# Attention kernel with a pipelined step: scores, transposes together, attention last, and one image's phi/g products taken into the start

## The chip, the cores and the metric

The kernel runs on one core of one Trainium2 chip. The metric is the device time of one execution in microseconds (us); the median of three runs of the kernel before is 183.82 us.

## The reference

The input is `x`, four images of 128 channels by 32 x 32 = 1024 pixels, in fp32. Per image:

```
# first block (64 inner channels)
g = Wg x + bg;  theta = Wt x + bt;  phi = Wp x + bp          # 64 x 1024 each
y = ((theta^T phi) / 1024) g^T                               # no softmax
z = x + Wo y^T + bo                                          # 128 x 1024
# second block (128 channels)
t = Wt2 z + bt2;  p = Wp2 z + bp2
attn = softmax(t^T p / sqrt(128))                            # 1024 x 1024, row by row
out = z + Wc (z attn^T) + bc
```

The first block has no softmax, so the kernel multiplies it out as one 128 x 128 matrix per image: `A = I + Wo (g phi^T / 1024) Wt` and an offset `d`, and then z = A x + d. In the second block it uses one matrix U for both projections, and V = Wc z for the values. The row terms `rho` replace the part of the bias that differs between rows.

## The kernel before

**Tiles.** A tile is 128 of the 1024 pixel rows of one image's attention matrix. There are 8 tiles an image and 32 in all (`ALL`), numbered n, with n = 8 b + t. Four tiles make a group, whose 512 columns are attended together into the PSUM bank `numer`.

**Precision.** Products that need nearly full fp32 are made of three fp32r matmuls of hi and lo parts (`three`, L220). Each hi part is written by ScalarE and the lo part is the difference, taken by VectorE after it.

**A tile's way through the engines.** TensorE writes the scores of tile n into `ring` (2 buffers, L296; 6 matmuls of 512 columns). VectorE takes the row maxima (`row_max`, L659). GpSimd adds the row terms (`row_shift`, L794). ScalarE takes the exponentials and their sum (`exps`, L511). VectorE multiplies by the reciprocal of the sum (`norm`, L665). TensorE transposes the tile in two halves of four 128 x 128 blocks (`turn`, L312) into `turned`, two PSUM banks, one per half, with one buffer. ScalarE copies each half as `PT_hi` (`high_turned`, L519), and VectorE writes `PT_lo` (`low_turned`, L673), which frees the half's bank. At last TensorE multiplies the group's tiles with the values, in four pieces of 6 matmuls over the next four steps (`attend`, L322).

**Jobs.** Between these, in the steps of image b, the preparation of image b+1 is made. It is cut into jobs, two a step at most (`job_one`, `job_two`): phi/g products (`pg0`, `pg1`, t = 1), their product `MT` and then `R` (t = 2), `A` and `Z0` (t = 3), `Z1` (t = 4), queries `t0` and values `V0` (t = 5), `V1`, `V2` (t = 6), `t1` (t = 7). All jobs write one PSUM bank, `aux`. The semaphore `aux_free` counts how often it was emptied; a job waits for the count that `aux_before` gives. Copies of `aux` are made by ScalarE, by VectorE, or by both in turn (A, t0, t1, V0 to V2: ScalarE writes the hi part, VectorE then the lo part and frees the bank).

**Order.** The order on each engine is written out by hand; each engine goes through its list strictly, with waits on semaphores. In step n, until n = 30, these are

```
TensorE:  scores(n+2), turn(n,0), job_one, attend piece, turn(n,1), job_two          L433-444
VectorE:  row_max(n+2), low_turned(n-1,1), low_turned(n,0), job_one, norm(n+1), job_two
ScalarE:  high_turned(n,0), job_one, exps(n+2), high_turned(n,1), copy_numer, job_two
GpSimd:   row_shift(n+2), then finish / high_x, low_x, split_z (parts of image b+1)
```

There is no attention in steps 0 to 3, since the first group isn't complete, and no job in image 3's steps (n of 24 and more). `copy_numer` (L528) empties `numer` every fourth step. On GpSimd, `high_x` comes at t = 0, `low_x` at t = 1 and 2, `split_z` at t = 4 and 5, and `finish` at t = 0 and 6; these are ops of 0.6 to 1.5 us. At n = 26 it also makes `V_last`, a 1024-column op.

**The start** (L348 to L394) makes image 0's preparation, with the first products of phi and g in the score ring, and then the scores of tiles 0 and 1; `numer` serves there as a spare bank for two of the three value parts of image 0. The last tile has a way of its own after the loop (L447 to L462).

**Transfers.** SyncE's queue loads the two halves of image 0, the weights, image 1 (L187), and then images 2 and 3 (`load`, L189) once their buffer is free; it then stores the results.

Of the kernel before, what the change touches and what calls it, by code (L numbers as in the profile page):

```python
# [12 lines left out]
IMAGES = 4  # L13
C = 128
# [4 lines left out]
ALL = IMAGES * TILES  # L19
# [31 lines left out]


JOBS = ("pg0", "pg1", "MT", "R", "A", "Z0", "Z1", "t0", "V0", "V1", "V2", "t1")
FIRST_JOBS = ("MT", "R", "A", "t1", "V2")


def aux_before(b, job):

    return len(FIRST_JOBS) + (b - 1) * len(JOBS) + JOBS.index(job) if b else FIRST_JOBS.index(job)

# [4 lines left out]


SPLIT_JOBS = ("A", "t0", "V0", "V1", "V2", "t1")
FIRST_SPLIT = ("t1", "V2")


def high_after(b, job):

    return (len(FIRST_SPLIT) + (b - 1) * len(SPLIT_JOBS) + SPLIT_JOBS.index(job) if b
            else FIRST_SPLIT.index(job)) + 1


def build(nc, x, pg_weights, pg_bias, inner, weights, out):
    with ExitStack() as ctx:
# [103 lines left out]
        def _(sp):  # L182
# [6 lines left out]
            def load(b):  # L189
                if b == 2:  # L190
                    sp.wait_ge(first_z, HALVES)
                else:
                    sp.wait_ge(aux_free, aux_after(b - 2, "pg1"))
                    sp.wait_ge(x_lo, (b - 2) * HALVES)
                sp.dma_start(X[:, b % 2, :], x[b]).then_inc(x_loaded[b], 16)
# [23 lines left out]
        def _(pe):  # L219
# [121 lines left out]
            def attend_last(j):  # L341
# [4 lines left out]
                return mm  # L346

            pe.wait_ge(idle_ready, 1)  # L348
            for _ in range(WARM_UP):
                nc.tensor.matmul(aux[:, 0:C], idle[:, :], idle[:, :], start=True, stop=True)  # L350
            pe.wait_ge(pg_w_loaded, 16)
# [28 lines left out]
            for half in range(HALVES):  # L380
                nc.tensor.matmul(ring[:, 1, columns(half)], AT[:, :], X[:, 0, columns(half)],
                                 start=True, stop=True).then_inc(first_z, 1)

            pe.wait_ge(u_lo, 1)
            pe.wait_ge(first_z_lo, 1)
            queries(0, first_t_bank(0), FIRST_T[0]).then_inc(first_t, 1)
            scores(0)
            pe.wait_ge(first_z_ready, 1)
            pe.wait_ge(vw_ready, 2)
            pe.wait_ge(conv_loaded, 16)  # L390
            value_chunks(0, numer, 0).then_inc(first_v, 1)
            queries(0, first_t_bank(1), FIRST_T[1]).then_inc(first_t, 1)
# [7 lines left out]

            def job_one(b, t):
                if t == 0 and b == 1:
                    first_value_part()
                if t == 1:
                    job_pg(b, 0)
# [12 lines left out]

            def job_two(b, t):
                if t == 0 and b == 1:  # L420
                    job_V(0, 2)
                if t == 1:
                    job_pg(b, 1)
                if t == 2:
                    job_R(b)
                if t == 3:
                    job_Z(b, 0)
                if t == 5:
                    job_V(b, 0)
                if t == 6:  # L430
                    job_V(b, 2)

            for n in range(ALL - 1):  # L433
                b, t = divmod(n, TILES)
                if n + 2 < ALL:
                    scores(n + 2)
                turn(n, 0)
                if b + 1 < IMAGES:
                    job_one(b + 1, t)
                if n >= GT:  # L440
                    attend(n // GT - 1, n % GT)
                turn(n, 1)
                if b + 1 < IMAGES:
                    job_two(b + 1, t)
            attend(ALL_GROUPS - 2, PIECES - 1)
# [20 lines left out]
        def _(act):  # L466
# [99 lines left out]

            def job_one(b, t):
                if t == 0 and b == 1:
# [13 lines left out]

            def job_two(b, t):
                if t == 0 and b == 1:
# [10 lines left out]
            for n in range(ALL - 1):  # L595
                b, t = divmod(n, TILES)
                high_turned(n, 0)
                if b + 1 < IMAGES:
                    job_one(b + 1, t)
                if n + 2 < ALL:  # L600
                    exps(n + 2)
                high_turned(n, 1)
                if n >= GT and n % GT == GT - 1:
                    copy_numer(n // GT - 1)
                if b + 1 < IMAGES:
                    job_two(b + 1, t)
            copy_numer(ALL_GROUPS - 2)
# [6 lines left out]
        def _(dve):  # L614
# [105 lines left out]
            first_z_low(1)  # L720
            first_t_low(0)
            row_max(0)
            dve.wait_ge(u_copied, 1)
# [6 lines left out]

            def job_one(b, t):
                if t == 0 and b == 1:
                    first_row_terms(1)
                    first_v_low(1)
                if t == 1:
                    make_pg(b, 0)
# [8 lines left out]

            def job_two(b, t):
                if t == 0 and b == 1:
                    low_V(0, 2)
                if t == 1:
                    make_pg(b, 1)  # L750
# [17 lines left out]
            low_turned(ALL - 2, 1)  # L768
            dve.wait_ge(turned_ready, ALL * HALVES)
# [117 lines left out]
```

## Time and profile before

| | |
|---|---|
| runs | 184.03, 182.73, 183.82 us; median 183.82 |
| the profiled execution | 183.74 us; its span 181.9 us, so 1.8 us lie around the span |
| mean granted TensorE clock | 0.991 |
| TensorE busy | 168.2 us, 92% |
| VectorE busy | 132.8 us, 73% |
| ScalarE busy | 98.0 us, 54% |
| GpSimd busy | 49.6 us, 27% |

A matmul's listed duration covers its whole way through the array and overlaps the next one's; the distance between the starts of two rows says what it costs TensorE. "Busy" therefore says little about slack; idle time in brackets at a row, with what ended it, says more.

### The profile page before, as it was taken

The page shows a single profiled execution, that of the slowest core. Times are in us where ns is not written, and L with a number is a line of the kernel's source. Part 1 is how long each engine was busy: PE and PEld are TensorE (multiplying, and loading weights), DVE is VectorE, ACT ScalarE, POOL GpSimd, SP SyncE. Part 2 cuts the span into 40 slices and gives each one's busy share as a digit, 9 for nine tenths or more (in the row PEclk, how much of TensorE's full clock was granted, in tenths as well). Part 3 has the DMA queues.
Part 4 walks back from the last instruction along what each step waited for, and adds up shares of the span by engine and source line. Part 5 has one row for each costly group of instructions (what it writes and reads, how often), then busy time and mean ns, then how long its engine had stood idle before and what let it go on. Part 6 is the DMA issues. An engine that isn't in the chain of part 4 may idle for free.

```text
span 181.9 us, 2601 instructions
## 1 busy us (share of the span) xinstructions
PE 168.2 (92%) x967; PEld 135.3 (74%) x967; DVE 132.8 (73%) x217; ACT 98.0 (54%) x178; POOL 49.6 (27%) x73
## 2 busy tenths in 40 slices
PE   7896896797999999999999999999999999898994
PEld 6755684675787878878787878788787867675794
DVE  1313697776999888756988889766988988988612
ACT  3032546357676665347666755557655856576320
POOL 1015012330440036210443063301523042403020
PEclk9997899999999999999999999999999999999999
DMA  4603000011000001000001010000001010000111
GB/s 133 184 0 115 0 4 0 0 48 73 0 2 0 0 4 58 0 0 4 0 0 58 0 49 14 0 0 0 4 0 61 0 58 4 0 0 0 58 61 58
DMA packets 2829, 4.76 MB, mean 26 GB/s; under 512 B 448, under 2 KB 1280, under 8 KB 2816
## 3 DMA queue, kind: packets, MB, share of 16 engines
q1 hardware_dynamic: 2304, 4.39, 6.9%
q10 hardware_dynamic: 512, 0.20, 0.6%
q8 instruction: 8, 0.13, 0.3%
q14 instruction: 5, 0.04, 0.1%
HBM read 2.49 MB, written 2.10 MB: 25 GB/s over the span
## 4 chain that ended last, share of the span: by engine, by line
PE 70%; DVE 23%; ACT 2%; DMA 2%; issue 1%; ACTq 0%
PE numer L337 14%; PE turned L318 11%; DVE negmax L662 10%; PE ring L223 8%; PE ring L225 8%; PE ring L224 8%; DVE PT_lo L677 7%; PE aux L229 3%; PE aux L282 3%; PE aux L344 2%; DMA pg_w<-pg_weights_dram 2%; PE aux L223 2%; DVE P L670 2%; PE ring L229 2%; PE aux L235 2%; PE aux L224 2%
## 5 line engine op out<-in xcount | busy, mean ns | idle before, releaser
L524 ACT ACTIVATE PT_hi<-turned 128x512 fp32r<-128x512 f32 x62 | 37.0, 596 | 40.0 <-PE turned L318 39.7
L662 DVE TENSOR_REDUCE negmax<-ring 128x1 f32<-128x1024 f32 x32 | 39.2, 1223 | 21.8 <-PE ring L225 21.2
L318 PE MATMUL turned<-identity,P 128*128 128x128 f32 x256 | 39.1, 276 | 5.5 <-DVE P L670 3.1
L318 PEld LDWEIGHTS turned<-identity,P 128*128 128x128 f32 x256 | 30.5, 140 | 17.5 <-DVE PT_lo L677 5.9
L516 ACT ACTIVATE P<-ring,shift 128x1024 f32<-128x1024 f32 x32 | 35.7, 1116 | 13.1 <-POOL shift L803 12.8
L803 POOL TENSOR_SCALAR shift<-negmax,rho 128x1 f32<-128x1 f32 x32 | 11.8, 368 | 106.4 <-DVE negmax L662 103.1
L677 DVE TENSOR_TENSOR PT_lo<-turned,PT_hi 128x512 fp32r<-128x512 f32 x62 | 39.8, 681 | 1.0 <-ACT PT_hi L524 0.9
L670 DVE TENSOR_SCALAR P<-P,rden 128x1024 f32<-128x1024 f32 x32 | 30.6, 957 | 1.1
L223 PE MATMUL ring<-Z_hi,t_hi 128*128 128x512 f32 x64 | 28.0, 438 | 1.5 <-DVE t_lo L707 1.5
L225 PE MATMUL ring<-Z_lo,t_hi 128*128 128x512 f32 x64 | 25.7, 402 | 0.0
L224 PE MATMUL ring<-Z_hi,t_lo 128*128 128x512 f32 x64 | 25.6, 400 | 0.0
L337 PE MATMUL numer<-PT_hi,V_hi 128*128 128x512 f32 x56 | 23.8, 424 | 0.0
L337 PE MATMUL numer<-PT_hi,V_lo 128*128 128x512 f32 x56 | 22.1, 395 | 0.0
L337 PE MATMUL numer<-PT_lo,V_hi 128*128 128x512 f32 x56 | 22.1, 395 | 0.0
L223 PEld LDWEIGHTS ring<-Z_hi,t_hi 128*128 128x128 f32 x64 | 12.2, 191 | 4.3 <-DVE t_lo L707 2.1
L225 PEld LDWEIGHTS ring<-Z_lo,t_hi 128*128 128x128 f32 x64 | 12.3, 192 | 2.9
L224 PEld LDWEIGHTS ring<-Z_hi,t_lo 128*128 128x128 f32 x64 | 12.3, 192 | 1.7
L337 PEld LDWEIGHTS numer<-PT_hi,V_lo 128*128 128x128 f32 x56 | 10.5, 188 | 2.5
L337 PEld LDWEIGHTS numer<-PT_hi,V_hi 128*128 128x128 f32 x56 | 10.6, 188 | 1.8
L337 PEld LDWEIGHTS numer<-PT_lo,V_hi 128*128 128x128 f32 x56 | 10.6, 189 | 1.6
L830 POOL TENSOR_TENSOR result<-attended,Z 128x512 f32<-128x512 f32 x7 | 9.0, 1287 | 5.4 <-ACT attended L534 5.4
L282 PE MATMUL aux<-VW,Z 128*128 128x130 f32 x52 | 8.1, 287 | 0.5 <-DVE V_lo L649 0.5
(113 smaller groups left out, 198.6 us busy)
## 6 DMA issues: line engine op xcount, KB each, us to landing
out_dram<-result SPq DMA_DIRECT2D x7, 256.0 KB, 2.0
X<-x_dram SPq DMA_DIRECT2D x3, 512.0 KB, 3.2
X<-x_dram SPq DMA_DIRECT2D x2, 256.0 KB, 4.1
out_dram<-result SPq DMA_DIRECT2D x1, 192.0 KB, 1.9
w<-weights_dram SPq DMA_DIRECT2D x1, 128.0 KB, 5.5
wi<-inner_dram ACTq DMA_DIRECT2D x1, 64.2 KB, 5.6
pg_w<-pg_weights_dram ACTq DMA_DIRECT2D x1, 64.0 KB, 3.6
pg_b<-pg_bias_dram ACTq DMA_DIRECT2D x1, 64.0 KB, 5.2
```

The costliest lines, as they stand in the source:

```text
L223: nc.tensor.matmul(to, left_hi, right_hi[:, cols], start=first, stop=False)
L224: nc.tensor.matmul(to, left_lo, right_hi[:, cols], start=False, stop=False)
L225: return nc.tensor.matmul(to, left_hi, right_lo[:, cols], start=False, stop=last)
L282: mm = nc.tensor.matmul(bank[:, at:at + V_COLS], Z[:, b % Z_BUFFERS, j * TILE:(j + 1) * TILE], VW[:, :], start=True, stop=True)
L318: mm = nc.tensor.transpose(turned[:, j * TILE:(j + 1) * TILE], P[:, n % P_BUFFERS, j * TILE:(j + 1) * TILE], identity[:, :])
L337: mm = nc.tensor.matmul(numer[:, :], left[:, b % 2, chunk], right[:, g, j, :], start=(j == 0 and n == 0), stop=(j == TILES - 1 and n == 2))
L516: nc.scalar.activation(P[:, n % P_BUFFERS, :], ring[:, n % 2, :], ACT.Exp, bias=shift[:, t:t + 1], accum_out=den[:, t:t + 1]).then_inc(pro ...
L524: nc.scalar.activation(PT_hi[:, group % GROUPS, half_chunks(half), k * TILE:(k + 1) * TILE], turned[:, columns(half)].rearrange("p (j r) - ...
L662: nc.vector.tensor_reduce(negmax[:, t:t + 1], ring[:, n % 2, :], AX.X, ALU.max, negate=True).then_inc(max_ready, 1)
L670: nc.vector.tensor_scalar(P[:, n % P_BUFFERS, :], P[:, n % P_BUFFERS, :], rden[:, t:t + 1], None, ALU.mult).then_inc(probs_normed, 1)
L677: nc.vector.tensor_tensor(PT_lo[:, group % GROUPS, half_chunks(half), rows], turned[:, columns(half)].rearrange("p (j r) -> p j r", j=CHUN ...
L803: nc.gpsimd.tensor_scalar(shift[:, t:t + 1], negmax[:, t:t + 1], rho[:, b % 2, t:t + 1], rho[:, b % 2, t:t + 1], ALU.subtract, ALU.add).th ...
```

## The change

In each step TensorE now makes scores(n+2), the first job, both halves of turn(n), the second job, and the attention piece last. VectorE makes row_max(n+2), the first job, norm(n+1), low_turned(n,0), the second job and low_turned(n,1). ScalarE makes the first job, both halves of high_turned(n), the second job and exps(n+2); copy_numer moved from the end of one step to the beginning of the next. GpSimd's program is the same.

Image 1's phi/g products leave step 1. Their first half is issued on TensorE after image 0's Z products, ahead of the first queries; the second half goes to the bank `numer`, between the first queries and scores(0). VectorE copies both (`make_pg(1, 0)`, `copy_pg`) between `first_t_low(0)` and `row_max(0)`. The numbering of the jobs is now a list, in which (1, pg0) stands behind (0, A); a value part that writes `numer` waits for the copy. The load of image 3 waits on the renamed counts. WARM_UP stays; `keep_warm` is only its loop as a function.

```diff
+AUX_ORDER = ([(0, "MT"), (0, "R"), (0, "A"), (1, "pg0"), (0, "t1"), (0, "V2")] + [(1, job) for job in JOBS[2:]]
+             + [(b, job) for b in range(2, IMAGES) for job in JOBS])
+SPLIT_ORDER = [(b, job) for b, job in AUX_ORDER if job in ("t0", "V0", "V1", "V2", "t1") or (job == "A" and b)]
...
# SyncE, load(3)
-                    sp.wait_ge(aux_free, aux_after(b - 2, "pg1"))
+                    sp.wait_ge(first_pg_copied, HALVES + 1)
+                    sp.wait_ge(aux_free, aux_after(1, "pg0"))
...
# TensorE, start
+            job_pg(1, 0)
             pe.wait_ge(u_lo, 1)
             pe.wait_ge(first_z_lo, 1)
             queries(0, first_t_bank(0), FIRST_T[0]).then_inc(first_t, 1)
+            phi_g_chunks(1, numer, 1).then_inc(first_pg, 1)
             scores(0)
...
+            pe.wait_ge(first_pg_copied, HALVES + 1)
             value_chunks(0, numer, 0).then_inc(first_v, 1)
...
# TensorE, step
                     scores(n + 2)
+                if b + 1 < IMAGES:
+                    early_job(b + 1, t)
                 turn(n, 0)
+                turn(n, 1)
                 if b + 1 < IMAGES:
-                    job_one(b + 1, t)
+                    late_job(b + 1, t)
                 if n >= GT:
                     attend(n // GT - 1, n % GT)
-                turn(n, 1)
-                if b + 1 < IMAGES:
-                    job_two(b + 1, t)
...
# ScalarE, step
+                if n >= 2 * GT and n % GT == 0:
+                    copy_numer(n // GT - 2)
+                if b + 1 < IMAGES:
+                    early_job(b + 1, t)
                 high_turned(n, 0)
+                high_turned(n, 1)
                 if b + 1 < IMAGES:
-                    job_one(b + 1, t)
+                    late_job(b + 1, t)
                 if n + 2 < ALL:
                     exps(n + 2)
-                high_turned(n, 1)
-                if n >= GT and n % GT == GT - 1:
-                    copy_numer(n // GT - 1)
-                if b + 1 < IMAGES:
-                    job_two(b + 1, t)
...
# VectorE, start
             first_t_low(0)
+            make_pg(1, 0)
+            dve.wait_ge(first_pg, HALVES + 1)
+            copy_pg(numer[:, :], 1, first_pg_copied)
             row_max(0)
...
# VectorE, step
                     row_max(n + 2)
-                if n >= 1:
-                    low_turned(n - 1, 1)
+                if b + 1 < IMAGES:
+                    early_job(b + 1, t)
+                norm(n + 1)
                 low_turned(n, 0)
                 if b + 1 < IMAGES:
-                    job_one(b + 1, t)
-                norm(n + 1)
-                if b + 1 < IMAGES:
-                    job_two(b + 1, t)
+                    late_job(b + 1, t)
+                low_turned(n, 1)
```

The jobs are the same as before under new names (`early_job` for `job_one`, `late_job` for `job_two`), except that phi/g is made only for b > 1.

## Rows read from the trace of the kernel before

**Rows 1.** The page: the chain that ended last, shares by engine.
```profile
PE 70%; DVE 23%; ACT 2%; DMA 2%; issue 1%; ACTq 0%
```
**Rows 2.** Busy time by stretch: image 1's eight steps, then step 26.
```profile
63.47:103.13 39.66, 39.42 (x231) 32.02 (x230) 32.28 (x53) 24.46 (x45) 13.10 (x17) 1.00 0.04 14
...
150.70:154.66 3.96, 3.89 (x23) 2.96 (x22) 3.23 (x6) 2.36 (x5) 0.96 (x2) 1.00 0.01 4
```
**Rows 3.** Timeline of step 8, which has no job: start, duration, instruction, [idle before].
```profile
63.47 0.48 PE L223 MATMUL ring<-Z_hi,t_hi 128*128 128x512 f32 x1
...
64.94 0.60 PE L318 MATMUL turned<-identity,P 128*128 128x128 f32 x4
65.13 1.23 DVE L662 TENSOR_REDUCE negmax<-ring 128x1 f32<-128x1024 f32 x1 [0.41 <-PE ring L225]
65.29 0.48 PE L337 MATMUL numer<-PT_hi,V_hi 128*128 128x512 f32 x1
...
65.63 0.60 ACT L524 ACTIVATE PT_hi<-turned 128x512 fp32r<-128x512 f32 x1 [0.70 <-PE turned L318]
...
66.27 1.28 DVE L677 TENSOR_TENSOR PT_lo<-turned,PT_hi 128x512 fp32r<-128x512 f32 x2
...
66.46 0.37 POOL L803 TENSOR_SCALAR shift<-negmax,rho 128x1 f32<-128x1 f32 x1 [3.98 <-DVE negmax L662]
...
67.01 0.66 PE L318 MATMUL turned<-identity,P 128*128 128x128 f32 x4
67.42 0.48 PE L223 MATMUL ring<-Z_hi,t_hi 128*128 128x512 f32 x1
```
**Rows 4.** Busy time by stretch, the start: columns PE, PEld, DVE, ACT, POOL, PEclk, DMA.
```profile
9.00:11.50 2.50, 2.30 (x18) 1.93 (x18) 0.42 (x1) 0.76 (x4) 0.00 (x0) 1.00 0.00 0
...
12.50:15.80 3.30, 1.54 (x7) 0.60 (x5) 1.85 (x3) 1.74 (x3) 1.96 (x4) 1.00 0.37 129
15.79:19.44 3.65, 3.64 (x12) 3.05 (x13) 0.85 (x1) 0.00 (x0) 1.02 (x1) 0.53 0.07 29
```
**Rows 5.** Timeline of the start: scores(0), the first value part, the next queries.
```profile
15.80 0.62 PE L223 MATMUL ring<-Z_hi,t_hi 128*128 128x512 f32 x1 [0.90 <-DVE t_lo L707]
...
18.35 1.37 PE L282 MATMUL numer<-VW,Z 128*128 128x130 f32 x6
...
19.47 0.42 PE L223 MATMUL turned<-Z_hi,UT_hi 128*128 128x384 f32 x1
```
**Rows 6.** Timeline of step 1, TensorE with its waits.
```profile
29.58 0.66 PE L318 MATMUL turned<-identity,P 128*128 128x128 f32 x4 [1.30 <-DVE P L670]
...
30.57 1.16 PE L229 MATMUL aux<-pg_w,X 128*128 128x128 f32 x8 [0.33 <-DVE V_lo L649]
```
**Rows 7.** Busy time by stretch: steps 1, 2 and 3.
```profile
26.66:34.40 7.74, 5.00 (x33) 3.74 (x32) 6.57 (x14) 4.67 (x10) 2.96 (x4) 1.00 0.00 0
34.40:38.90 4.50, 4.10 (x36) 3.15 (x34) 3.48 (x6) 1.85 (x4) 1.50 (x2) 1.00 0.00 0
38.90:44.14 5.24, 4.12 (x25) 3.35 (x25) 4.16 (x8) 3.35 (x9) 0.47 (x2) 1.00 0.32 105
```
**Rows 8.** Timeline of step 13: t0's hi and lo copies, then V0.
```profile
91.08 0.69 ACT L496 ACTIVATE t_hi<-aux,U 128x512 fp32r<-128x512 f32 x1
...
92.08 0.74 DVE L638 SCALAR_TENSOR_TENSOR t_lo<-aux,U,t_hi 128x512 fp32r<-128x512 f32 x1
...
92.88 0.94 PE L282 MATMUL aux<-VW,Z 128*128 128x130 f32 x6
...
93.57 0.48 PE L223 MATMUL ring<-Z_hi,t_hi 128*128 128x512 f32 x1
```
**Rows 9.** Busy time by stretch: steps 13 and 14.
```profile
88.07:93.57 5.50, 5.50 (x33) 4.22 (x31) 5.36 (x7) 3.86 (x8) 3.24 (x4) 1.00 0.00 0
93.57:98.77 5.20, 5.04 (x33) 4.18 (x32) 4.53 (x10) 3.25 (x6) 1.62 (x2) 1.00 0.00 0
```
**Rows 10.** Timeline of step 12: a GpSimd op and VectorE's norm beside it.
```profile
87.80 1.29 POOL L822 TENSOR_TENSOR Z_lo<-Z,Z_hi 128x512 fp32r<-128x512 f32 x1
...
87.92 1.72 DVE L670 TENSOR_SCALAR P<-P,rden 128x1024 f32<-128x1024 f32 x1
```
**Rows 11.** Busy time by stretch: step 27, then steps 29 and 30.
```profile
154.66:159.34 4.68, 3.90 (x24) 2.96 (x22) 4.64 (x7) 2.42 (x5) 2.19 (x2) 1.00 0.00 0
163.30:172.40 9.10, 8.03 (x43) 5.92 (x41) 7.29 (x13) 4.75 (x9) 1.60 (x2) 1.00 0.07 29
```
**Rows 12.** The tile P: VectorE's norm, min/median/max ns.
```profile
L670 DVE TENSOR_SCALAR P<-P,rden x32: 752/754/2122, 22.2 to 170.6; 128x1024 f32<-128x1024 f32 x32
```

More of the change, by code:

```diff
@@ L53 @@
 JOBS = ("pg0", "pg1", "MT", "R", "A", "Z0", "Z1", "t0", "V0", "V1", "V2", "t1")
-FIRST_JOBS = ("MT", "R", "A", "t1", "V2")
+AUX_ORDER = ([(0, "MT"), (0, "R"), (0, "A"), (1, "pg0"), (0, "t1"), (0, "V2")] + [(1, job) for job in JOBS[2:]]
+             + [(b, job) for b in range(2, IMAGES) for job in JOBS])
+SPLIT_ORDER = [(b, job) for b, job in AUX_ORDER if job in ("t0", "V0", "V1", "V2", "t1") or (job == "A" and b)]
 def aux_before(b, job):
-    return len(FIRST_JOBS) + (b - 1) * len(JOBS) + JOBS.index(job) if b else FIRST_JOBS.index(job)
+    return AUX_ORDER.index((b, job))
 def aux_after(b, job):
     return aux_before(b, job) + 1
-SPLIT_JOBS = ("A", "t0", "V0", "V1", "V2", "t1")
-FIRST_SPLIT = ("t1", "V2")
 def high_after(b, job):
-    return (len(FIRST_SPLIT) + (b - 1) * len(SPLIT_JOBS) + SPLIT_JOBS.index(job) if b
-            else FIRST_SPLIT.index(job)) + 1
+    return SPLIT_ORDER.index((b, job)) + 1
 def build(nc, x, pg_weights, pg_bias, inner, weights, out):
@@ L346, in attend_last, with keep_warm @@
                 return mm
+            def keep_warm(to, count):
+                for _ in range(count):
+                    nc.tensor.matmul(to, idle[:, :], idle[:, :], start=True, stop=True)
             pe.wait_ge(idle_ready, 1)
-            for _ in range(WARM_UP):
-                nc.tensor.matmul(aux[:, 0:C], idle[:, :], idle[:, :], start=True, stop=True)
+            keep_warm(aux[:, 0:C], WARM_UP)
             pe.wait_ge(pg_w_loaded, 16)
@@ L399, in first_value_part, with early_job @@
                 value_chunks(0, numer, 1).then_inc(first_v, 1)
-            def job_one(b, t):
+            def early_job(b, t):
                 if t == 0 and b == 1:
                     first_value_part()
-                if t == 1:
+                if t == 1 and b > 1:
                     job_pg(b, 0)
@@ L417, in job_one, with late_job @@
                     job_t(b, 1)
-            def job_two(b, t):
+            def late_job(b, t):
                 if t == 0 and b == 1:
                     job_V(0, 2)
-                if t == 1:
+                if t == 1 and b > 1:
                     job_pg(b, 1)
@@ L565, in _, with early_job @@
             exps(1)
-            def job_one(b, t):
+            def early_job(b, t):
                 if t == 0 and b == 1:
@@ L581, in job_one, with late_job @@
                     high_t(b, 1)
-            def job_two(b, t):
+            def late_job(b, t):
                 if t == 0 and b == 1:
@@ L729, in _, with early_job @@
             low_t(0, 1)
-            def job_one(b, t):
+            def early_job(b, t):
                 if t == 0 and b == 1:
@@ L734, in job_one @@
                     first_v_low(1)
-                if t == 1:
+                if t == 1 and b > 1:
                     make_pg(b, 0)
@@ L744, in job_one, with late_job @@
                     low_t(b, 1)
-            def job_two(b, t):
+            def late_job(b, t):
                 if t == 0 and b == 1:
                     low_V(0, 2)
-                if t == 1:
+                if t == 1 and b > 1:
                     make_pg(b, 1)
@@ L759, in _ @@
                     row_max(n + 2)
-                if n >= 1:
-                    low_turned(n - 1, 1)
+                if b + 1 < IMAGES:
+                    early_job(b + 1, t)
+                norm(n + 1)
                 low_turned(n, 0)
                 if b + 1 < IMAGES:
-                    job_one(b + 1, t)
-                norm(n + 1)
-                if b + 1 < IMAGES:
-                    job_two(b + 1, t)
-            low_turned(ALL - 2, 1)
+                    late_job(b + 1, t)
+                low_turned(n, 1)
             dve.wait_ge(turned_ready, ALL * HALVES)
```

## The prediction

> **What bounds the kernel now.** I read the chain of waits first, then busy time by stretch, then the timelines. The chain is 70% TensorE and 23% VectorE [rows 1]: look for where VectorE comes in. In image 1's eight steps TensorE was idle 0.24 of 39.66 us [rows 2]; image 2 repeats them. No order can gain there except by packing matmuls closer. The idle time lies at both ends: steps 1 to 3 have 2.74, 0.40 and 1.12 us [rows 7], the start runs partly at the low clock [rows 4], and image 3's steps, which have no jobs, are paced by VectorE [rows 2, 11].
>
> **A step without jobs.** In step 8 scores take 1.47 us (63.47 to 64.94), a half of the transposes 0.35, attention again 1.47, to 66.76; then turn(n,1) waits until 67.01 [rows 3], because low_turned(n-1,1) stands behind row_max(n+2) on VectorE. The work is 3.95 - 0.25 = 3.7 us. In the new order tile n's lo copies end in step n. With S the start of scores: row maximum at S+1.6 (1.66 here, less the changeover after transposes), norm from S+2.8, to 3.7, lo copies to 4.3 and 4.95; the next transposes start at S+3.7+1.4 = 5.1, and their second half at 5.5. So TensorE waits for nothing. VectorE needs 1.14 + 0.95 + 2 x 0.6 = 3.3 us a step [rows 3, 12], less than 3.7. The step becomes 3.7, as TensorE's work is unchanged.
>
> **Image 3 and the end.** Steps 24, 25, 26 and 28 take 3.96 each, alike within 0.01 [rows 2], 27 takes 4.68, 29 and 30 together 9.10 [rows 11]: 29.62 us. New: 5 x 3.7 = 18.5. From step 29, counted from S: its work ends at 3.7; turn(30) waits for tile 29's lo copies (4.3 and 4.95), ends at 5.35, and 12 attention matmuls (2 x 1.47, less a changeover) end at 8.2. That is 26.7, a gain of **2.9**. Step 8 and step 16 gain 0.25 each.
>
> **Steps with two jobs.** This is the price. The second job needs `aux` empty. Before, turn(n,0)'s remainder, attention and a half of the transposes lay between the jobs; now only eight transposes, 0.85 us, and attention is queued behind the waiting job. Also row_max(n+2) stands ahead of the first job's copy on VectorE. At t = 5: t0 is issued S+1.4 to 2.07, ScalarE's copy follows 2.3 to 3.0 (0.69), VectorE's 3.05 to 3.8 (0.74) [rows 8]; transposes end at 2.95, V0 starts at 3.85, so TensorE idles 0.9. V0 takes 0.69 (92.88 to 93.57), attention 1.4: 5.93 against 5.50, **+0.43** [rows 8, 9]. At t = 6 V1's copies (0.5 and 0.8 us, from 2.4 and 2.9) let V2 go at 3.7: 5.65 against 5.20, **+0.45** [rows 9]. At t = 1 pg0's copy waits for row_max until 2.75 and takes 0.7; pg1 goes at 3.45, 0.35 late; the step is 5.8, +0.15. At t = 2 MT and R need ScalarE alone, which is free early: -0.1. At t = 3 AT_lo is ready at 3.1, 0.2 late, which the two changeovers saved pay for: 0. One job at t = 4 and 7: 0. Image 1 then costs 39.66 + 0.15 - 0.1 + 0.43 + 0.45 - 0.25 = 40.35, **+0.7**, image 2 the same: **+1.4**. In steps 4 to 7 of image 0 it is **+0.9**. VectorE's backlog after t = 5 (its last lo copy ends near S+7.1 to 7.5) is gone before the next row maximum at 5.93+1.6.
>
> **Steps 0 to 3.** Times here are on the old trace's scale. In step 0 the value part moves before the transposes and the step grows by 0.5: scores(3) starts at 27.1 instead of 26.66. VectorE's list gives row_max(2) 25.5 to 26.7, value part to 28.05, norm(1) to 29.0, lo copies of tile 0 at 29.6 and 30.7 (V2's copy between). So turn(1,0) starts at 29.65, 1.1 us idle, against 29.58 before [rows 6], but turn(1,1) follows at 30.75 with no phi/g products (16 matmuls, two lots of 0.85) and no copies between, and scores(4) starts at 31.25 instead of 34.40: -3.15. Step 2 is 3.8 (old 4.50), bounded by TensorE; step 3 is 4.6 against 5.24, as AT_lo stands behind a VectorE list that is 1.2 us late and Z0 waits 0.85 for it. By scores(6): 39.65 against 44.14, so **-4.4**.
>
> **The start.** All loads are in: the DMA share is 0.00 from 9.00 to 11.50 [rows 4], so image 1 is there. Two times eight passes of 0.11 us go into the 1.76 us that TensorE idles in 12.50 to 15.80 [rows 4]: the first lot 13.15 to 14.25, ahead of queries at 14.37; the second 14.75 to 15.65, ahead of scores(0) at 15.80 [rows 5]. Tight, up to 0.1 late. VectorE's two copies (1.4 us) lie between 15.74 and row_max(0). They cost nothing in their cover; without it the 0.7 us of the second would show in V's wait. More matters: after the thinly used stretch (1.54 busy of 3.30) the clock fell, and was 0.53 in 15.79 to 19.44, the 1.2 GHz level [rows 4]. There scores(0) took 2.55 (15.80 to 18.35) and the value part 1.12 [rows 5], against 1.4 and 0.69 at 2.4 GHz [rows 3, 8]: 1.6 us. With the gap two thirds filled I take it that the clock stays up: **-1.5**; if it falls anyway, 0. The Trainium skill (TensorE: Matmul & The Clock Gate, "The HAM clock gate") has the fall follow an idle window; the trace agrees only in part, since the engine was busy nearly half of the time ahead of the fall. By it the gain would stand as well.
>
> **The sum.** -4.4 + 0.9 + 1.4 - 2.9 - 1.5 = -6.5. The profiled execution took 183.74 us, 0.08 under the median of 183.82; 183.82 - 6.5 = **177.3**, the forecast.
>
> **Unknown: norm beside GpSimd.** A norm lasts 0.75 us, but 1.72 when a GpSimd op of 1.29 us began just ahead of it [rows 10, 12]. Before, row_shift and norm stood apart; now both are released by the end of row_max, within 0.1 us of each other, and GpSimd's longer ops follow row_shift directly. If norm gets in first, shift is late by up to 0.75, which exps, at the end of ScalarE's list, can bear: 0. If GpSimd keeps its turn, norm is late by 0.37, or by 0.37 + 1.29. I take the first, since nothing held norm in step 8, with a third of the norms at risk as the bound.
> The Trainium skill (GPSIMD Engine Reference, "Specifications") says that the two engines share SBUF interfaces and contend when VectorE runs in a two-port mode; the trace agrees (1.72 against 0.75), and this rule speaks against the change.
>
> **Rivals.**
> - *The clock falls anyway* (free of the filling): 177.3 + 1.5 = 178.8. For it: the fall came after a partly busy stretch. Chance 0.15.
> - *Second jobs wait longer than walked.* I count 2.2 us of waits an image at t = 1, 3, 5 and 6. If VectorE comes to each first job 0.3 to 0.5 late, 11 such steps add 3.3 to 5.5: 180.6 to 182.8. For it: VectorE has 5.36 us of work in step 13 [rows 9]. Chance 0.15, half of it above 182.
> - *Slower: GpSimd holds norm.* Place: norm behind row_shift and the op after it, in t = 0, 1, 2, 4, 5 and 6 of three images, 18 steps. Price 1.66 each on VectorE, of which a light step absorbs 0.4; up to 1 us a step reaches TensorE, +18. It decides from 6.5/18 = 0.36 us a step; beyond 0.46 the kernel is slower than 185.7. Against it: the second ops were mostly off norm's path, and waits for jobs absorb some. Chance 0.08, near 187.
> - *More gained:* the waits of second jobs are covered by packing, under 175.5. Chance 0.07.
>
> **The numbers.** The forecast's own case has 0.55 and spans 175.6 to 179.5. The range from 175.5 to 181.5 takes in the clock case and the lower half of the waits case; about 0.2 is left out. About 1% (182.0 and 185.7) is what a measurement can tell from no change. Faster: 0.55 + 0.15 + 0.07 + half of 0.15 = 0.84. Same: 0.08. Slower: 0.08.
>
> **What would show it.** In the changed kernel's profile: PEclk full from 15.8 to 19.5 and scores(0) 1.4 long; scores(4) starting 4.6 earlier (-3.15 and -1.5); about 3.7 between scores in image 3; TensorE idle near 0.9 and 0.75 ahead of V0 and V2 with lo copies as releasers, images 1 and 2 at 40.35 each. Norms of 1.7 or more in most steps, transposes waiting for PT_lo, or images 1 and 2 above 42 us would make the prediction wrong.

## The result and the profile after

The changed kernel takes 177.69 us (177.53 to 177.83) against 183.27 in the same comparison, ratio 0.970 [0.964, 0.975]: 5.6 us faster, forecast 177.3. Its profiled execution took 177.83 us, 5.91 less than the one of before; its span is 175.9 us.

Where the time went, by the starts of scores in the two timelines (tail: to the first matmul of `attend_last`):

| stretch | before | after | difference | predicted |
|---|---|---|---|---|
| to scores(1) | 21.56 | 20.16 | -1.40 | -1.5 |
| scores(1) to scores(6), all of steps 0 to 3 | 22.58 | 17.57 | -5.01 | -4.4 |
| steps 4 to 7 | 19.33 | 20.50 | +1.17 | +0.9 |
| images 1 and 2 (steps 8 to 23) | 79.31 | 81.68 | +2.37 | +1.4 |
| image 3 and the end | 29.63 | 26.56 | -3.07 | -2.9 |
| sum | | | -5.94 | -6.5 |

The page of the changed kernel, the chain that ended last, by engine, answers to [rows 1]: VectorE's share fell from 23% to 18%.

```profile
PE 75%; DVE 18%; ACT 3%; DMA 2%; issue 1%; ACTq 0%
```

Busy time by stretch, image 1's eight steps and then its step 13 (columns PE, PEld, DVE, ACT, POOL, PEclk, DMA share, GB/s); they answer to [rows 2, 9]:

```profile
58.23:99.08 40.85, 39.34 (x230) 32.41 (x228) 33.20 (x53) 23.16 (x45) 14.26 (x17) 1.00 0.04 14
...
82.88:89.19 6.31, 5.53 (x31) 4.26 (x29) 4.68 (x7) 3.65 (x7) 3.60 (x5) 1.00 0.00 0
```

TensorE, idle 0.24 us there before, is now idle 1.5, and more than half of it (0.78) lies in step 13. A step without jobs, number 26, in the timeline (start, duration, instruction, [idle before]); it answers to [rows 3]:

```profile
147.24 0.39 PE L222 MATMUL ring<-Z_hi,t_hi 128*128 128x512 f32 x1
...
148.63 1.04 PE L317 MATMUL turned<-identity,P 128*128 128x128 f32 x8
148.84 1.22 DVE L667 TENSOR_REDUCE negmax<-ring 128x1 f32<-128x1024 f32 x1 [0.39 <-PE ring L224]
149.27 1.09 ACT L529 ACTIVATE PT_hi<-turned 128x512 fp32r<-128x512 f32 x2 [0.48 <-PE turned L317]
149.43 0.48 PE L336 MATMUL numer<-PT_hi,V_hi 128*128 128x512 f32 x1
...
150.16 0.91 POOL L810 TENSOR_SCALAR shift<-negmax,rho 128x1 f32<-128x1 f32 x1 [2.67 <-DVE negmax L667]
150.16 0.75 DVE L675 TENSOR_SCALAR P<-P,rden 128x1024 f32<-128x1024 f32 x1
...
150.83 0.68 DVE L682 TENSOR_TENSOR PT_lo<-turned,PT_hi 128x512 fp32r<-128x512 f32 x1
150.91 0.39 PE L222 MATMUL ring<-Z_hi,t_hi 128*128 128x512 f32 x1
```

Read it by starts: scores 1.39 us, eight transposes 0.80, attention 1.48, together 3.67, and no bracket on a TensorE row. Norm and row_shift start at the same time, 150.16; norm keeps its 0.75, row_shift takes 0.91 instead of 0.37. So it is in 15 of the 32 tiles, in which the two start within 0.07 us of each other. Seven other norms start 0.16 to 0.31 us behind one of GpSimd's longer ops and take 1.52 to 1.67 us; no TensorE row is shown waiting for them.

The start, by stretch and in the timeline, answers to [rows 4, 5]: the gap is full, the clock stays at its 2.4 GHz level, and scores(0) takes 1.50 us, the value part 0.58.

```profile
12.50:15.80 3.30, 3.30 (x22) 2.51 (x20) 1.71 (x3) 1.74 (x3) 1.96 (x4) 1.00 0.30 88
15.80:19.50 3.70, 3.70 (x21) 2.84 (x19) 2.69 (x6) 0.58 (x1) 1.57 (x2) 1.00 0.17 68
```
```profile
15.99 0.50 PE L222 MATMUL ring<-Z_hi,t_hi 128*128 128x512 f32 x1
...
17.49 0.83 PE L281 MATMUL numer<-VW,Z 128*128 128x130 f32 x6
...
18.07 0.42 PE L222 MATMUL turned<-Z_hi,UT_hi 128*128 128x384 f32 x1
```

Step 13 (t = 5) in the changed kernel's timeline answers to [rows 8]:

```profile
83.07 1.29 POOL L829 TENSOR_TENSOR Z_lo<-Z,Z_hi 128x512 fp32r<-128x512 f32 x1
...
84.51 0.47 PE L222 MATMUL aux<-Z_hi,UT_hi 128*128 128x512 f32 x1
...
85.49 0.69 ACT L501 ACTIVATE t_hi<-aux,U 128x512 fp32r<-128x512 f32 x1 [1.76 <-PE aux L224]
...
86.21 0.75 DVE L643 SCALAR_TENSOR_TENSOR t_lo<-aux,U,t_hi 128x512 fp32r<-128x512 f32 x1 [0.52 <-ACT t_hi L501]
...
87.02 0.94 PE L281 MATMUL aux<-VW,Z 128*128 128x130 f32 x6 [0.69 <-DVE t_lo L643]
```

Here is the price of the new order: V0 waits for t0's lo copy, with the attention piece behind it in the queue. Counted from starts, TensorE makes nothing for 0.94 us there: the eight transposes begin at 85.29 and take 0.79. And t0 itself starts late, at 1.63 us behind the start of the step, right after a GpSimd op that ends at 84.36.

### The profile page after: what moved, and what is told of

The parts are those of the page before. It is cut to its first block, busy times and chain, and to the rows that moved or that the text cites. A ratio compares the mean times of both kernels' runs of the same rounds, so it can differ in the third digit from the quotient of the medians.

```text
span 175.9 us, 2602 instructions
## 1 busy us (share of the span) xinstructions
PE 164.4 (93%) x967; PEld 136.1 (77%) x967; DVE 131.7 (75%) x217; ACT 94.5 (54%) x178; POOL 56.9 (32%) x73
## 4 chain that ended last, share of the span: by engine, by line
PE 75%; DVE 18%; ACT 3%; DMA 2%; issue 1%; ACTq 0%
PE numer L336 22%; PE turned L317 9%; PE ring L222 8%; DVE negmax L667 7%; PE ring L224 7%; PE ring L223 7%; PE aux L281 4%; PE aux L222 2%; PE aux L343 2%; DVE PT_lo L682 2%; DMA pg_w<-pg_weights_dram 2%; PE aux L228 2%; PE ring L228 2%; DVE P L675 2%; DVE t_lo L643 2%; PE aux L234 2%
## 5 line engine op out<-in xcount | busy, mean ns | idle before, releaser
L810 POOL TENSOR_SCALAR shift<-negmax,rho 128x1 f32<-128x1 f32 x32 | 20.0, 625 | 94.3 <-DVE negmax L667 83.5
L682 DVE TENSOR_TENSOR PT_lo<-turned,PT_hi 128x512 fp32r<-128x512 f32 x62 | 40.4, 682 | 0.4 <-ACT PT_hi L529 0.4
L529 ACT ACTIVATE PT_hi<-turned 128x512 fp32r<-128x512 f32 x62 | 33.7, 595 | 10.0 <-PE turned L317 10.0
L317 PE MATMUL turned<-identity,P 128*128 128x128 f32 x256 | 33.8, 274 | 1.8 <-DVE PT_lo L682 1.8
L317 PEld LDWEIGHTS turned<-identity,P 128*128 128x128 f32 x256 | 29.3, 141 | 5.6 <-DVE P L675 2.3
L675 DVE TENSOR_SCALAR P<-P,rden 128x1024 f32<-128x1024 f32 x32 | 29.8, 933 | 1.1
L222 PE MATMUL ring<-Z_hi,t_hi 128*128 128x512 f32 x64 | 25.6, 400 | 0.6 <-DVE t_lo L712 0.6
L224 PE MATMUL ring<-Z_lo,t_hi 128*128 128x512 f32 x64 | 25.1, 393 | 0.0
L336 PE MATMUL numer<-PT_hi,V_hi 128*128 128x512 f32 x56 | 24.3, 433 | 0.0
L501 ACT ACTIVATE t_hi<-aux,U 128x512 fp32r<-128x512 f32 x7 | 4.8, 689 | 11.2 <-PE aux L224 11.2
```

Source lines behind the costliest of these rows:

```text
L222: nc.tensor.matmul(to, left_hi, right_hi[:, cols], start=first, stop=False)
L224: return nc.tensor.matmul(to, left_hi, right_lo[:, cols], start=False, stop=last)
L317: mm = nc.tensor.transpose(turned[:, j * TILE:(j + 1) * TILE], P[:, n % P_BUFFERS, j * TILE:(j + 1) * TILE], identity[:, :])
L336: mm = nc.tensor.matmul(numer[:, :], left[:, b % 2, chunk], right[:, g, j, :], start=(j == 0 and n == 0), stop=(j == TILES - 1 and n == 2))
L529: nc.scalar.activation(PT_hi[:, group % GROUPS, half_chunks(half), k * TILE:(k + 1) * TILE], turned[:, columns(half)].rearrange("p (j r) - ...
L675: nc.vector.tensor_scalar(P[:, n % P_BUFFERS, :], P[:, n % P_BUFFERS, :], rden[:, t:t + 1], None, ALU.mult).then_inc(probs_normed, 1)
```

## The experiments

All are compared with the kernel before, which lay at 183.5 to 183.8 in the first three groups of runs and at 182.3 in the last, for the most part because of what the first experiment shows. "A clock of 1.0" is a run's mean granted TensorE clock of 0.999 or 1.000.

### 1. Only the gap filled (e1_warm_only)

```diff
+            pe.wait_ge(aux_free, aux_after(0, "A"))
+            for _ in range(10):
+                nc.tensor.matmul(numer[:, 0:C], idle[:, :], idle[:, :], start=True, stop=True)
             pe.wait_ge(u_lo, 1)
             pe.wait_ge(first_z_lo, 1)
             queries(0, first_t_bank(0), FIRST_T[0]).then_inc(first_t, 1)
+            for _ in range(8):
+                nc.tensor.matmul(numer[:, 0:C], idle[:, :], idle[:, :], start=True, stop=True)
             scores(0)
```

> The kernel before, with 10 and 8 matmuls on zeros put into the two gaps of the start (ahead of the first queries, and between them and scores(0)); nothing else is changed and the output is the same. Theory A (the clock falls because the engine is thinly used from 12.8 to 15.8 us): PEclk stays full until 20 us, scores(0) takes 1.4 instead of 2.55 us, scores(1) starts 1.4 to 1.6 us earlier, total about 181.8 (ratio 0.992). Rival B (the clock's fall has another cause, or zeros don't count as activity): clock 0.5 from 16 to 19.5 as before, total unchanged at 183.3.

182.26 us, ratio 0.996 [0.992, 0.999]; scores(1) at 20.10 (21.56 before).

```profile
12.50:15.80 3.30, 2.69 (x24) 1.67 (x22) 1.78 (x3) 1.74 (x3) 1.96 (x4) 1.00 0.34 92
15.80:19.50 3.70, 3.54 (x18) 2.81 (x18) 1.50 (x4) 0.60 (x2) 1.51 (x2) 1.00 0.15 60
```

Theory A: with the gap filled by matmuls on zeros the clock behind it stays full. The median moved only by 1.25, because in the kernel before the fall does not come every time: of its 29 runs beside this one 20 had a mean clock below 1.0, most of them 0.991, with a median of 183.74, and 9 a clock of 1.0, with 182.11. The fall costs 1.6 us, and how often it comes sets the median. With the gap filled 9 of 12 runs had a clock of 1.0.

The gap makes the fall possible and not certain. The trace of e6_last_only (experiment 5) has the start of the kernel before, with the same 1.54 us of work in 12.50 to 15.80, and a granted clock of 1.00 behind it; scores(0) takes 1.49 us there, and scores(1) starts at 19.87:

```profile
15.70 0.49 PE L223 MATMUL ring<-Z_hi,t_hi 128*128 128x512 f32 x1 [0.91 <-DVE t_lo L715]
...
17.19 0.83 PE L282 MATMUL numer<-VW,Z 128*128 128x130 f32 x6
```

Over all four groups of runs the kernel before had a clock of 1.0 in 22 of 70: 9 of 29, 7 of 23, 4 of 11 and 2 of 7. In the last group two of the five with a lower mean clock took 182.03 and 182.31 us, so not every fall costs 1.6 us, and its median of 182.31 comes from these. Where the clock fell is known for the profiled executions only.

### 2 and 3. Each half of the change alone (e2_pg_only, e3_order_only)

```diff
# e2_pg_only: the changed kernel, steps in the old order; TensorE shown, ScalarE and VectorE likewise
                     scores(n + 2)
+                turn(n, 0)
                 if b + 1 < IMAGES:
                     early_job(b + 1, t)
-                turn(n, 0)
+                if n >= GT:
+                    attend(n // GT - 1, n % GT)
                 turn(n, 1)
                 if b + 1 < IMAGES:
                     late_job(b + 1, t)
-                if n >= GT:
-                    attend(n // GT - 1, n % GT)
# e3_order_only: the changed kernel, phi/g of image 1 again in step 1
-            job_pg(1, 0)
...
-            phi_g_chunks(1, numer, 1).then_inc(first_pg, 1)
...
-                if t == 1 and b > 1:
+                if t == 1:
```

> The changed kernel with the old order of the steps on all three engines: only the phi/g products of image 1 are moved. Theory A: the clock stays up (-1.4), step 1 loses 16 matmuls, two VectorE copies and three of its four waits (-2.5 or so), images 1 to 3 as before (39.66 an image, 3.96 and 4.68 a step in image 3): 179.3. Rival C (the order is what gains, and moved products only fill a gap): step 1 keeps its waits, since VectorE's list sets them: 181.8, which is the clock alone.

181.86 us, ratio 0.992 [0.989, 0.995].

> The changed kernel with image 1's phi/g products back in step 1 (first job pg0, second job pg1), numbering as before. Theory A: clock falls as before; image 3's steps 3.66 (-3.2 in all), image 1 and 2 at 40.85 (+2.4), steps 4 to 7 +1.2, steps 1 to 3 -1.5 to -2.5: 181.3 to 182.5. Rival C: most of the gain is here, 179.5 or less. The gains of this run and of the one with the moved products alone add up to 5.6 by theory A; if they help each other, to less than 5.

180.55 us, ratio 0.987 [0.983, 0.991]. Theory A took it that the clock falls; the six runs in which it did have a median of 181.7, inside its range.

The moved products alone missed theory A by 2.5 us, and this looked like rival C. The trace says otherwise. TensorE's timeline, then two stretches, of e2_pg_only:

```profile
27.68 0.66 PE L317 MATMUL turned<-identity,P 128*128 128x128 f32 x4 [1.31 <-DVE P L675]
30.40 0.66 PE L317 MATMUL turned<-identity,P 128*128 128x128 f32 x4 [2.06 <-DVE PT_lo L682]
30.82 0.48 PE L222 MATMUL ring<-Z_hi,t_hi 128*128 128x512 f32 x1
```
```profile
26.00:30.40 4.40, 1.03 (x6) 0.42 (x4) 3.71 (x8) 2.71 (x7) 0.79 (x3) 1.00 0.00 0
30.40:33.90 3.50, 3.50 (x15) 2.62 (x15) 2.41 (x4) 1.62 (x3) 1.13 (x1) 0.66 0.00 0
```

With the products gone and the old order kept, the transposes of step 1 still wait for the lo copy, TensorE works 1.03 us of 4.40, and the clock, kept up at 16 us, falls at about 31.5, by when TensorE has been at work again for 1 us. Eleven of its 12 runs had a clock of 0.98 or 0.99; the one at 1.0 took 180.29. So this fall explains 1.5 us of the miss. Most of the rest is step 1: it went from 7.74 to 6.05 us, 1.7 less, where theory A said 2.5; that it became shorter at all speaks against rival C. In the kernel with the order alone 6 of 12 runs fell (181.7), 6 did not (179.8).

So the two gains must be compared at one clock. At 1.0: before 182.1, products alone 180.3 (one run; experiment 4 bears it out), order alone 179.8, both 177.7; that is -1.8, -2.3 and -4.4, which add up within 0.3. On the medians, against 183.5, they are -1.65 and -2.96, and both together -5.8: each half alone leaves room for a fall of the clock, and both together had none in four runs.

### 4. The second fall taken away (e5_pg_only_warm)

```diff
# e2_pg_only, and in step 1
                 turn(n, 0)
+                if n == 1:
+                    pe.wait_ge(first_v_lo, 2)
+                    keep_warm(numer[:, 0:C], 14)
```

> The kernel with only the moved products (old order of the steps), with 14 matmuls on zeros into the bank numer between the two halves of turn(1), where TensorE stood idle for 2.06 us and after which the clock fell for some 3.5 us. Nothing that is computed changes. Theory A (in that kernel a second fall of the clock, brought on by the longer idle stretch that the moved products left in step 1, takes back most of the start's gain): clock 1.0, 180.3 in nearly all runs, 1.5 less than without. Rival (the clock there has nothing to do with the gap, or the added matmuls delay the transposes as much): 181.8.

180.28 us, ratio 0.985 [0.980, 0.991]; three of 4 runs had a clock of 1.0, with 180.18 to 180.32; without these matmuls it was 1 of 12. The stretch that had 1.03 us of work now has 1.82 in 4.40, and the clock behind it is full:

```profile
26.00:30.40 4.40, 1.82 (x20) 1.25 (x18) 3.69 (x8) 2.71 (x7) 0.78 (x3) 1.00 0.00 0
30.40:33.90 3.50, 3.48 (x30) 2.94 (x30) 3.06 (x5) 2.23 (x4) 1.22 (x2) 1.00 0.00 0
```

### 5. The new order in image 3 alone (e6_last_only)

```diff
# the kernel before; TensorE shown, ScalarE and VectorE likewise
                 turn(n, 0)
+                if b == IMAGES - 1:
+                    turn(n, 1)
...
-                turn(n, 1)
+                if b < IMAGES - 1:
+                    turn(n, 1)
```

> The kernel before with the new order in image 3's steps alone (n of 24 and more), on all three engines; image 1's products stay in step 1. Theory A: these steps go from 3.96 (and 4.68) to 3.67, all else as before: 3.0 us less than the kernel before, 180.5 in the median, with images 1 and 2 still at 39.66 a piece. Rival (the gain at the end comes from what steps 0 to 23 hand over, as VectorE's backlog): less than 1 us.

181.82 us, ratio 0.990 [0.986, 0.994]; at a clock of 1.0, 180.6 against 182.1, so -1.5, half of theory A's. Steps 25 to 28 take 3.65 to 3.67 as foreseen, but step 24, the first, takes 5.45. In its timeline:

```profile
144.62 0.66 PE L318 MATMUL turned<-identity,P 128*128 128x128 f32 x4 [1.48 <-DVE PT_lo L685]
144.67 1.55 DVE L678 TENSOR_SCALAR P<-P,rden 128x1024 f32<-128x1024 f32 x1
```

Step 24 is 1.5 us longer than in the old order and 1.8 longer than the steps of the new one, once: tile 23's second lo copy, which the old order leaves for step 24 and behind the row maximum there, holds transposes that now come earlier. (The norm in the second row takes 1.55 because it starts behind a GpSimd op; no TensorE row of the step waits for it.) The gain belongs to the order, but an order can't be changed between steps for nothing.

### 6. norm moved behind a lo copy (e7_norm_later)

```diff
# the changed kernel, VectorE
-                norm(n + 1)
                 low_turned(n, 0)
+                norm(n + 1)
```

> The changed kernel with VectorE's norm(n+1) behind low_turned(n,0), so that it no longer starts together with GpSimd's row_shift. Theory A (norm, started 0.1 us earlier, holds row_shift from 0.37 to 0.92 us, which delays split_z, and by it t0 at t = 5 by 0.24): row_shift 0.37 in most steps, t0 without a gap, an image's steps 0.2 to 0.3 shorter, total 177.0. Rival E (row_shift's delay is hidden, and norm now meets GpSimd's longer ops instead): norm's mean above 1.0 us instead of 0.93, total 177.7 to 179.

181.91 us, ratio 0.994 [0.990, 0.997]: 4.2 us lost, more than either side said. Theory A's detail is right: row_shift takes 0.37 throughout, t0 follows scores at once (44.83 to 45.06), and the steps at t = 5 take 6.09 instead of 6.31. But norm's mean went from 933 to 1149 ns. At the end of step 26 and in step 27:

```profile
152.41 2.42 POOL L861 TENSOR_TENSOR V_last<-V_hi,V_lo 128x1024 f32<-128x1024 f32 x1
...
152.69 2.69 DVE L675 TENSOR_SCALAR P<-P,rden 128x1024 f32<-128x1024 f32 x1
...
155.43 1.25 PE L317 MATMUL turned<-identity,P 128*128 128x128 f32 x8 [1.06 <-DVE P L675]
```

A norm that starts 0.28 us behind a GpSimd op ends 0.55 us after it, and the transposes wait for the norm. It is the held norms that cost, not the later place in the list by itself: in image 3 a step behind a norm of 0.75 us takes 3.66 or 3.67, as in the changed kernel, one behind a norm of 1.59 takes 4.00, and the one behind the 2.69 takes 5.10. This is the mechanism of the prediction's rival "GpSimd holds norm"; in the changed kernel norm follows row_max and gets in first in every tile in which it is released together with row_shift.

### 7 and 8. Attention ahead of the second job (e4_attend_first, e10_attend_pe)

```diff
# both, TensorE
                 turn(n, 0)
                 turn(n, 1)
-                if b + 1 < IMAGES:
-                    late_job(b + 1, t)
                 if n >= GT:
                     attend(n // GT - 1, n % GT)
+                if b + 1 < IMAGES:
+                    late_job(b + 1, t)
# e4_attend_first also: ScalarE exps(n+2) ahead of late_job,
# VectorE low_turned(n, 1) ahead of late_job
```

> The changed kernel with the attention piece between the transposes and the second job on TensorE; on ScalarE exps(n+2) and on VectorE low_turned(n,1) now stand ahead of the second job's copies. Theory A (the second job waits for the first job's copies, 0.85 at t = 5 and 0.7 at t = 6, and attention waits behind it): no wait ahead of V0 and V2, an image's steps 39.4 instead of 40.85, total 173.5 to 175. Rival D (VectorE's work of 5.36 us at t = 5 is the bound, whatever the order): the wait moves to the first job of t = 6 or to the transposes, an image stays above 40.5, total 177 to 178.

175.40 us, ratio 0.958 [0.954, 0.962], 0.4 above theory A's range: V0 and V2 wait no longer, but V1 now does, and image 1 takes 39.81, not 39.4.

> The changed kernel with the attention piece ahead of the second job on TensorE alone; ScalarE and VectorE keep the changed kernel's lists (second job's copies ahead of exps(n+2) and of low_turned(n,1)). Theory A: the waits of 0.7 and 0.45 ahead of V0 and V2 are gone, but the second job's result now comes 1.4 us later and exps(n+2) and low_turned(n,1) stand behind it, so that the transposes of the next step wait for PT_lo in steps with two jobs: 176 to 178.5. Rival (the position on TensorE is all that matters): 175.4, as with all three lists changed.

172.80 us, ratio 0.944 [0.939, 0.949], with TensorE's list alone changed. I had expected the other two lists to have to follow; the contrary holds. No TensorE row of images 1 and 2 waits for PT_lo, as theory A had said it would; the late second job costs only at t = 7, where the step takes 4.82 instead of 4.36. Image 1's steps in e10_attend_pe:

```profile
56.65:95.77 39.12, 38.87 (x230) 32.09 (x229) 33.17 (x53) 23.06 (x45) 14.30 (x17) 1.00 0.04 14
```

The 40.85 of the changed kernel has become 39.12, also less than the 39.66 of before. Step 13 in its timeline, where V0 now follows the attention piece with no wait, and its lo copy still stands ahead of low_turned(n,1):

```profile
83.88 0.75 DVE L643 SCALAR_TENSOR_TENSOR t_lo<-aux,U,t_hi 128x512 fp32r<-128x512 f32 x1 [0.53 <-ACT t_hi L501]
...
85.22 0.83 PE L281 MATMUL aux<-VW,Z 128*128 128x130 f32 x6
...
86.95 0.54 DVE L654 TENSOR_TENSOR V_lo<-aux,V_hi 128x384 fp32r<-128x384 f32 x1
...
87.54 0.94 PE L281 MATMUL aux<-VW,Z 128*128 128x130 f32 x6
```

V_lo ends at 87.49, V1 starts at 87.54. In e4_attend_first V_lo is last, and V1 waits (VectorE's row, then TensorE's):

```profile
88.80 0.54 DVE L654 TENSOR_TENSOR V_lo<-aux,V_hi 128x384 fp32r<-128x384 f32 x1
```
```profile
89.39 0.82 PE L281 MATMUL aux<-VW,Z 128*128 128x130 f32 x5 [0.67 <-DVE V_lo L654]
```

### 9 and 10. Which list cost the 2.6 us (e11_pe_act, e12_pe_dve)

```diff
# e11_pe_act: e10_attend_pe, and ScalarE
+                if n + 2 < ALL:
+                    exps(n + 2)
                 if b + 1 < IMAGES:
                     late_job(b + 1, t)
-                if n + 2 < ALL:
-                    exps(n + 2)
# e12_pe_dve: e10_attend_pe, and VectorE
                 low_turned(n, 0)
+                low_turned(n, 1)
                 if b + 1 < IMAGES:
                     late_job(b + 1, t)
-                low_turned(n, 1)
```

> The kernel with the attention piece ahead of the second job on TensorE alone (172.8 us), and on ScalarE exps(n+2) ahead of the second job's copies. Theory A (the three lists differ in what a late copy holds up; on ScalarE it is R's copy, behind an exponential of 1.1 us, that A waits for at t = 3, and Z0's that Z1 waits for at t = 4): 1.0 and 0.25 us of waits in steps 3 and 4 of image 0, where no attention piece gives time, and little in images 1 and 2: 174.0 to 174.8. Rival (it is VectorE's list that cost the 2.6 us): 172.8.

> The kernel with the attention piece ahead of the second job on TensorE alone (172.8 us), and on VectorE low_turned(n,1) ahead of the second job's lo copies. Theory A (V0's lo copy, now last in the list of t = 5, holds V1, the first job of t = 6, by 0.67 us in each of images 1 and 2): step 14 is 5.7 instead of 5.1, 173.8 to 174.4. Rival (it is ScalarE's list that cost the 2.6 us): 172.8.

174.36 us, ratio 0.955 [0.948, 0.962], and 174.89 us, ratio 0.960 [0.952, 0.968]. Each costs something, and in the places foreseen: with ScalarE's list, A waits 0.69 for R and Z1 0.24 for Z0 in image 0; with VectorE's, V1 waits 0.66 in step 6 and 0.67 in steps 14 and 22. With ScalarE's list there are two more waits in image 0 that I had not foreseen: turn(1,1) waits 0.75 for a lo copy (0.34 in e10_attend_pe) and scores(8) wait 0.66, shown as "issue". For e12_pe_dve I had left out step 6, of image 0, which is most of the 0.5 us by which it came out above its range. The two costs (1.6 and 2.1 us) are more than the 2.6 of both lists together, so they hide one another in part.

### 11 and 12. The value jobs moved (e8_v0_early, e9_v_spread)

Both start from e4_attend_first.

```diff
# e8_v0_early, on the three engines, with V0 ahead of t0 in the job list
-                if t == 5:
+                if t == 4:
                     job_V(b, 0)
# e9_v_spread, on the three engines, with t1 ahead of V2 in the job list
-                if t == 6:
-                    job_V(b, 1)            # first job
...
                 if t == 6:
-                    job_V(b, 2)
+                    job_V(b, 1)            # second job
+                if t == 7:
+                    job_V(b, 2)
```

> The kernel with the attention piece ahead of the second job, and V0 moved from t = 5, where VectorE had 5.4 us of work, to t = 4, where it had 2.7 and there was no second job; in the job list V0 stands before t0. Theory A (in t = 5 to 7 VectorE's work, bunched, is what is left above TensorE's own work): the wait of 0.67 ahead of V1 is gone, the four steps t = 4 to 7 take 18.8 instead of 20.2, an image 38.4, total 171 to 172. Rival F (the waits come from the order of the copies, not from the amount of work in one step): an image stays at 39.5, total 174.5 to 175.4.

> The kernel with the attention piece ahead of the second job, and the value jobs spread: V0 stays second job at t = 5, V1 becomes the second job of t = 6 (which has no first job now), V2 the second job of t = 7; in the job list t1 stands before V2. Theory A (what is left in t = 5 to 7 is that V1, as first job, needs V0's lo copy, the last on VectorE's list of the step before, and waits 0.67): no wait ahead of a first job at t = 6, the three steps take 14.6 to 15 instead of 15.8, total 172.5 to 173.3. Rival G (every lo copy at the end of VectorE's list is late for the next step's first job, so the wait comes back ahead of t1 at t = 7): 15.6 or more, total 175.4. Rival H (norm held by GpSimd's finish at t = 6): V1's copies late as before, wait over 0.5 at t1.

175.97 us, ratio 0.960 [0.956, 0.964], and 175.95 us, ratio 0.960 [0.956, 0.965]: both predictions of theory A failed, by 4 and 3 us. In e8_v0_early V1's wait is gone (step 14 takes 4.78, in e4_attend_first 5.72), but step 13 is no shorter (5.41 against 5.30). Its end is a wait of scores(16), shown as "issue"; by the times it is for Z's lo part, which GpSimd ends at 87.90:

```profile
86.62 1.28 POOL L829 TENSOR_TENSOR Z_lo<-Z,Z_hi 128x512 fp32r<-128x512 f32 x1
...
88.01 0.47 PE L222 MATMUL ring<-Z_hi,t_hi 128*128 128x512 f32 x1 [0.56 <-issue]
```

and the wait for V_lo comes back ahead of t1 (0.56). In e9_v_spread V1 has no wait, and t1 at t = 7 waits 0.95 instead; the three steps take 15.7 us. Spreading work was the wrong cure: what a job waited for was the position of one copy in VectorE's list, which e10_attend_pe had right. Rival G describes it, though the total is 0.6 above its 175.4.

## Why the prediction was right, and where it was off

The forecast of 177.3 is 0.4 from the 177.69 that was measured, and that close it is in part by luck: steps 0 to 3 gained 0.6 more than the sum has, and the steps with two jobs cost 1.2 more.

**The start.** Right in mechanism and size for an execution in which the clock falls (-1.40, predicted -1.5). But the forecast took the fall as given from one profile, and the median of before is a mixture: at a clock of 1.0 throughout the kernel before takes 182.1, and the change is worth 4.4 there, and 5.6 to 5.8 against the median. The forecast of the time itself does not suffer by it. The term is all clock. From the first Z product to scores(0) it is 4.25 us in the traces of before, of e6_last_only (old start, no fall) and of the changed kernel, so the moved products were free. From there to scores(1) it is 5.76 with the fall and 4.17 in both others. The fall costs 1.59; of this 0.19 does not show in the table, because the changed kernel's first Z product started that much later.

The Trainium skill (TensorE: Matmul & The Clock Gate, "HAM oscillation — how this bites in real kernels") describes a clock that falls again after waits inside a kernel. e2_pg_only shows one, with 1.03 us of work in 4.40 ahead of it.

**Steps 0 to 3.** -5.01 against -4.4. The walk through step 1 held: turn(1,0) still waits (0.88 us, walk 1.1), turn(1,1) 0.34, and the products are gone. Step 2 took 4.02, not 3.8, and step 3 took 4.13, not 4.6: Z0 waited 0.18 and not 0.85, since VectorE's list was less late than I had it (its row maximum started 1.81 us into step 3, 0.2 later than in a step on time, and not 1.2).

**Steps with two jobs.** Right in mechanism: V0 and V2 wait for lo copies with attention queued behind (0.69 and 0.49 us in the brackets). e10_attend_pe shows it by one edit on one engine: with attention ahead of the second job the two steps t = 5 and 6 of image 1 take 5.31 and 5.10 instead of 6.31 and 5.53 (before: 5.50 and 5.20), and the image 39.12. The size was 0.5 an image too small. The term that was mis-sized is t = 5: 6.31, not 5.93. Of the 0.38, 0.22 goes back to norm and row_shift starting together, for without that (e7) the step takes 6.09: row_shift takes 0.92 at t = 4, split_z comes later by as much, and t0, which needs Z_lo, starts 0.24 late. Another 0.08 is attention, which took 1.48 and not 1.4. I had written that exps could bear a late row_shift, which is so, and had not asked what else stands behind it on GpSimd.

**Image 3.** -3.07 against -2.9, five steps at 3.67. Four of these steps gained 0.3 each by VectorE's list, as I had it. Step 27 gained 1.01, and for that I had given no reason. Its 4.68 us in the kernel before were a norm held by GpSimd's `V_last`:

```profile
154.03 2.45 POOL L854 TENSOR_TENSOR V_last<-V_hi,V_lo 128x1024 f32<-128x1024 f32 x1
...
154.90 2.12 DVE L670 TENSOR_SCALAR P<-P,rden 128x1024 f32<-128x1024 f32 x1
...
157.08 0.66 PE L318 MATMUL turned<-identity,P 128*128 128x128 f32 x4 [0.79 <-DVE P L670]
```

In the changed kernel this norm starts with row_shift, at 150.16, and `V_last` only at 151.04. So 0.7 of the 3.07, what step 27 took over the other steps before, comes from norm getting in ahead of GpSimd's long op.

**norm beside GpSimd.** Taken as 0 by the guess that norm gets in first. Where the two are released together it does, in all 15 tiles; seven norms were held by longer ops all the same, and no TensorE wait is put down to them. e7_norm_later measured what the other outcome costs, 4.2 us.

The Trainium skill (SBUF — State Buffer, "SBUF: two separate sides") has the pair of SBUF ports that VectorE and GpSimd share as an exclusive lock, which whichever op starts first keeps for its whole length. The trace agrees in both directions, and in size within 0.2 us: row_shift 0.91 beside a norm, norm 2.69 beside a GpSimd op, each about 0.2 less than its own time and what was left of the other's.

**The rivals.** The clock did not fall. Second jobs did not wait longer than walked: by the starts 0.94 us ahead of V0 (walk 0.9) and 0.72 ahead of V2 (0.75), and VectorE was not late for t0, for it stood idle 0.52 us ahead of t_lo, waiting for t_hi. The steps are 1.2 us longer than the sum has because t0 itself started late, for the larger part. No step of the changed kernel is shown to be slower by a held norm.

Open: what decides in an execution of the kernel before whether the clock falls (it did not in 22 of 70, and the three chips used hardly differ), and why norm, and not row_shift, gets in first where the two start within some hundredths of a microsecond, as in those 15 tiles.

## What to carry to other kernels

In a queue that is worked through in order, put between two jobs that share a buffer the piece of work that needs neither of them; what stands behind a waiting job pays for the wait too. Write down for every copy who needs its buffer next, and give the front of the copying engine's list to the one that is needed first, before spreading work evenly. Compare kernels by their clock as well as by their medians: a gap filled in one place can open another behind which the clock falls, so that two halves of a change look as if they added up to less than the whole.

## What the runs showed of the hardware

- The same program's TensorE clock can fall in one execution and not in the next. In the profiled one of before it was 0.53 in 15.79 to 19.44, near its 1.2 GHz level, after TensorE had worked 1.54 us of 3.30 [rows 4]; in the trace of e6_last_only it stayed at the 2.4 GHz level after the same start. Of 29 executions of the kernel before 20 had a mean clock below 1.0 and 9 did not, with medians of 183.7 and 182.1 us. With that gap filled by matmuls on zeros scores(0) ran at the 2.4 GHz level, and 9 of 12 executions had a clock of 1.0.
- VectorE's norm and a GpSimd op that meet hold one another up: the one that starts first keeps its time (norm 0.75 us), the other's is longer by what is left of the first, less about 0.2 us (row_shift 0.37 to 0.91 beside a whole norm; norm 0.75 to 2.69 beside a GpSimd op with 2.14 us to go, and to 1.72 beside one with 1.17 to go [rows 10]).
